# A gated attention and mixture-of-experts layer on one core: where the passages between its stages put five small pieces of work

## The reference, cut to what matters

```
x = x + tanh(g_xattn) * attention(layernorm(x), ctx)       # q, k, v, o of 512 x 512
n = layernorm(x)
probs = softmax(n @ gate_w.T)                              # 8 experts
g, m = top_k(probs per expert, k = 2 * 2048 / 8 = 512)     # 512 tokens for each expert and batch
h = gelu(n[m] @ w1[e])                                     # 512 x 512 by 512 x 2048
out = scatter_add(g * (h @ w2[e]))                         # 512 x 2048 by 2048 x 512
x = x + tanh(g_ffn) * out
```

## Time and profile before

| | us |
|---|---|
| median of 3 runs | 1557.32 |
| lowest and highest | 1556.76, 1558.54 |
| the profiled execution | 1556.92 |
| its span, first to last instruction | 1555.2 |

### The profile page before, as it was taken

The page is one execution under the profiler, slowest core; times in us unless marked ns, Lnnn a source line. Parts: engine busy times, 40 slices in busy tenths (PEclk is TensorE's granted clock), DMA queues, the critical chain, the costliest instruction groups (busy, mean ns, idle before and its releaser), DMA issues.

```text
span 1555.2 us, 20287 instructions
## 1 busy us (share of the span) xinstructions
PE 1498.2 (96%) x7329; PEld 1230.2 (79%) x7329; DVE 1016.6 (65%) x1714; ACT 721.5 (46%) x1270; POOL 589.4 (38%) x554
## 2 busy tenths in 40 slices
PE   6987699999999999999999999999999999999997
PEld 6765477787788888888888888888888888888886
DVE  2677676657766676676667666667667665766543
ACT  2244433355444554454445554554445444554432
POOL 2264555534544044323443244404432344323311
PEclk9998799999999999999999999999999999999999
DMA  7274623533342333344233423334324423342133
GB/s 230 76 242 158 203 89 118 135 127 85 86 123 58 105 88 102 95 88 116 82 109 73 117 78 113 66 97 101 96 89 88 116 81 109 79 111 73 49 71 79
DMA packets 101385, 163.37 MB, mean 105 GB/s; under 512 B 7411, under 2 KB 45315, under 8 KB 101285
## 3 DMA queue, kind: packets, MB, share of 16 engines
q1 hardware_dynamic: 86885, 128.50, 26.5%
q0 software_dynamic: 14400, 33.56, 11.5%
HBM read 128.48 MB, written 33.55 MB: 104 GB/s over the span
## 4 chain that ended last, share of the span: by engine, by line
PE 88%; DVE 7%; DMA 2%; issue 1%; ACT 1%; POOL 1%; SPq 0%; POOLq 0%; DVEq 0%; ACTq 0%
PE bank L1408 42%; PE bank L1294 33%; PE bank L1268 4%; PE bank L1585 2%; PE bank L565 1%; DVE atleast L971 1%; DVE onehot L1468 1%; DMA x_s<-in_x 1%; PE bank L406 1%; PE bank L589 1%; DVE x L840 1%; DVE hid_low L1286 0%; DMA ctx_raw<-in_ctx 0%; PE bank L1457 0%; PE bank L554 0%
## 5 line engine op out<-in xcount | busy, mean ns | idle before, releaser
L1408 PE MATMUL bank<-w2hl,hh 128*128 128x512 f32 x2024 | 628.8, 392 | 0.0
L1294 PE MATMUL bank<-xo,whl 128*128 128x512 f32 x2352 | 544.0, 390 | 3.5 <-DVE mix L1358 2.8
L1294 PEld LDWEIGHTS bank<-xo,whl 128*128 128x128 f32 x2352 | 442.0, 188 | 97.3 <-DVE mix L1358 3.7
L1408 PEld LDWEIGHTS bank<-w2hl,hh 128*128 128x128 f32 x2024 | 376.2, 188 | 75.3
L1408 PE MATMUL bank<-w2hl,hid_low 128*128 128x512 f32 x1012 | 394.0, 389 | 0.0
L1408 PEld LDWEIGHTS bank<-w2hl,hid_low 128*128 128x128 f32 x1012 | 190.1, 188 | 39.8
L1532 POOL DMA_INDIRECT layer_out<-y,slot_row x64 | 104.6, 1634 | 296.7 <-ACT y L1447 281.3
L1222 POOL TENSOR_TENSOR whl<-raw,whl 128x512 fp32r<-128x512 f32 x56 | 81.3, 1452 | 261.1 <-ACT whl L1188 261.1
L1253 DVE TENSOR_TENSOR w2hl<-raw,w2hl 128x512 fp32r<-128x512 f32 x213 | 147.8, 716 | 40.6 <-ACT w2hl L1248 40.6
L1248 ACT ACTIVATE w2hl<-raw 128x512 fp32r<-128x512 f32 x228 | 136.5, 624 | 58.9 <-DMA raw<-in_L_ffn_w 40.1
L1227 POOL TENSOR_TENSOR whl<-wsum,whl 128x512 fp32r<-128x512 f32 x56 | 73.9, 1319 | 183.5 <-ACT whl L1209 183.5
(11 more groups left out here) (230 smaller groups left out, 1792.1 us busy)
## 6 DMA issues: line engine op xcount, KB each, us to landing
raw<-in_L_ffn_w SPq DMA_DIRECT2D x228, 256.0 KB, 2.7
raw<-in_L_ffn_w SPq DMA_DIRECT2D x72, 512.0 KB, 4.9
x_s<-in_x SPq DMA_DIRECT2D x8, 1024.0 KB, 9.5
layer_out<-x SPq DMA_DIRECT2D x8, 1024.0 KB, 10.4
xn_rows<-xn SPq DMA_DIRECT2D x8, 1024.0 KB, 5.2
raw_k<-in_L_xattn_Wk SPq DMA_DIRECT2D x1, 1024.0 KB, 5.5
raw_q<-in_L_xattn_Wq SPq DMA_DIRECT2D x1, 1024.0 KB, 11.3
raw_v<-in_L_xattn_Wv SPq DMA_DIRECT2D x1, 1024.0 KB, 13.4
```

What stands on the lines that cost most here:

```text
L1294: last = pe.matmul(bk[:, :], whl[:, p % 2, part, 2 * w + k, :], xo[:, xpart, x, k, :], start=(not adds and k == 0 and part == HIGH and xpa ...
L1408: last = pe.matmul(Y_BANKS[c][:, :], high if hpart == HIGH else low[:, c * P:(c + 1) * P], w2hl[:, f % 4, part, :], start=(s == 0 and hpar ...
```

## The change

It makes five edits.

1. The low part of w1 pair 0 goes from GpSimd, where it stood ahead of the gathers, to VectorE, ahead of the token splits. The function is renamed `w1_low_part` and takes the engine; GpSimd's low part of pair 1 waits until that of pair 0 is made.
2. On GpSimd the deviations of quarter 6 stand ahead of the four gathers; those of quarter 7 stay behind them.
3. On VectorE the logits of quarters 6 and 7 stand ahead of the fourth chunk's split.
4. TensorE makes the second batch's first count in the output stage of block 0, after its first quarter, like the others; `hidden_pe` loses its parameter.
5. At the change from expert 0 to expert 1, ScalarE's copy of the first product stands behind the high part of w1 pair 1 and ahead of the high part of its sums, and VectorE's low parts of expert 1's first two w2 blocks stand behind its output rows.

```diff
--- before.py
+++ after.py
@@ -766,14 +766,13 @@
                         rows(q, i)
 
 
-            w1_low_pool(pool, 0, 0, 0)
+            deviations(NQ - 2)
             for c in range(NC):
                 gather_pool(pool, 0, 0, c)
-            deviations(NQ - 2)
             deviations(NQ - 1)
             for f in range(2):
                 w2_low_sub(pool, 0, 0, f)
-            w1_low_pool(pool, 0, 0, 1)
+            w1_low_part(pool, 0, 0, 1)
             for q in (NQ - 2, NQ - 1):
                 for i in range(Q):
                     rows(q, i)
@@ -894,10 +893,12 @@
                     mean_out(q)
                 between(q, 3)
                 between(q, 4)
-            for c in range(NC):
+            w1_low_part(dve, 0, 0, 0)
+            for c in range(NC - 1):
                 split_tokens_dve(dve, 0, c)
             logits_out(NQ - 2)
             logits_out(NQ - 1)
+            split_tokens_dve(dve, 0, NC - 1)
 
         def attention_over(eng):
 
@@ -1208,7 +1209,10 @@
             act.wait_ge(w1_sums, pairs_before(e, p) * 3 + 3)
             act.activation(whl[:, p % 2, HIGH, 2 * S1:14, :], wsum[:, :, :], ACT.Copy).then_inc(w1_sum_high, 1)
 
-        def w1_low_pool(pool, e, b, p):
+        def w1_low_part(pool, e, b, p):
+
+            if is_plain(e) and b == 0 and p == 1:
+                pool.wait_ge(w1_low, 1)
             high, low = whl[:, p % 2, HIGH, :, :].bitcast(F32), whl[:, p % 2, LOW, :, :]
             pool.wait_ge(w1_high, pair_no(e, b, p) + 1)
             if is_plain(e):
@@ -1255,7 +1259,7 @@
 
 
 
-        def hidden_pe(pe, b, f, inside=None):
+        def hidden_pe(pe, b, f):
             n = step_no(0, b, f)
             p = f // 2
             if f == 0:
@@ -1269,8 +1273,6 @@
                                      xp[:, b, xpart, k, :],
                                      start=(k == 0 and part == HIGH and xpart == HIGH),
                                      stop=(k == KD - 1 and part == LOW))
-                if k == 1 and inside is not None:
-                    choice_pe(pe, 1, inside)
             last.then_inc(h_sum, 1)
 
         def gelu_act(act, b, f):
@@ -1630,7 +1632,7 @@
         OPERANDS_2 = {7: 0, 9: 1, 11: 2, 13: 3}
 
         def choice_piece(b, f):
-            return f if b == 0 and 1 <= f < N_PIECES else None
+            return f if b == 0 and f < N_PIECES else None
 
         def next_pair(b, f):
 
@@ -1653,7 +1655,7 @@
             for b in range(B):
                 for f in range(KF):
                     if f + 1 < KF:
-                        hidden_pe(pe, b, f + 1, 0 if b == 0 and f == 0 else None)
+                        hidden_pe(pe, b, f + 1)
                     if b == 0:
                         if f == SLOTS_1:
                             slots_pe(pe, 1)
@@ -1680,6 +1682,8 @@
                         operands_high_act(act, 1, OPERANDS_2[f])
                     if f % 2 == 0:
                         w1_high_act(act, *next_pair(b, f))
+                        if b == 1 and f + 2 == KF:
+                            copy_p1_act(act, 1, 0)
                         if next_pair(b, f)[0] == 1:
                             w1_sum_high_act(act, 1, next_pair(b, f)[2])
                     if b == 0 and f == LAST_SLOT:
@@ -1690,7 +1694,6 @@
                 if b == 0:
                     gelu_act(act, 1, 0)
                 else:
-                    copy_p1_act(act, 1, 0)
                     hidden_act(act, 1, 0)
                 for c in (0, 1):
                     output_rows(act, 0, b, c, y_act)
@@ -1698,7 +1701,7 @@
         def plain_dve(dve, own):
             for b in range(B):
                 for f in range(KF):
-                    if choice_piece(b, f) is not None:
+                    if f > 0 and choice_piece(b, f) is not None:
                         choice_dve(dve, own, 1, choice_piece(b, f))
                     if f + 1 < KF:
                         split_hidden_dve(dve, b, f + 1)
@@ -1707,7 +1710,8 @@
                     if b == 1 and f in OPERANDS_2:
                         operands_mix_dve(dve, 1, OPERANDS_2[f])
                     if b == 1:
-                        w2_low_sub(dve, *next_block(b, f))
+                        if next_block(b, f)[0] == 0:
+                            w2_low_sub(dve, *next_block(b, f))
                     else:
                         if f == HOT_1:
                             hot_dve(dve, 0, 1)
@@ -1731,6 +1735,9 @@
                     combine_dve(dve, 1, 0)
                 for c in (2, 3):
                     output_rows(dve, 0, b, c, y_dve)
+                if b == 1:
+                    for f in range(2):
+                        w2_low_sub(dve, 1, 0, f)
 
         def plain_pool(pool):
             for b in range(B):
@@ -1740,7 +1747,7 @@
                     if w2_no(*next_block(b, f)) < W2_EARLY:
                         w2_low_sub(pool, *next_block(b, f))
                     if f % 2 == 0:
-                        w1_low_pool(pool, *next_pair(b, f))
+                        w1_low_part(pool, *next_pair(b, f))
                     if b == 0 and f == GATHER_1:
                         for c in range(NC):
                             gather_pool(pool, 0, 1, c)
@@ -1869,7 +1876,7 @@
             for p in range(NP):
                 new = following_pair(e, p, final)
                 if new is not None:
-                    w1_low_pool(pool, new[0], 0, new[1])
+                    w1_low_part(pool, new[0], 0, new[1])
                 if p == 2:
                     promote_pool(pool, e, 1)
                 if p in GATHER_AT and not final:
```

## The result

| | before | after |
|---|---|---|
| median of 6 runs each, on one chip | 1557.87 | 1547.12 |
| lowest and highest | 1555.69, 1558.56 | 1545.97, 1548.93 |
| the profiled execution | 1556.92 | 1545.97 |
| its span | 1555.2 | 1543.9 |

The ratio is 0.9934, with a 95% interval of 0.9921 to 0.9947: 10.3 us less by the ratio (8.3 to 12.3). The forecast was 1547.5. Five further runs of the same kernel, beside nine more runs of the kernel before, had a median of 1548.59 and a ratio of 0.9944 (0.993 to 0.9957), which is 8.7 us less.

A forecast was written before the change was run, and what follows sets the result against it. TensorE, 88% of the chain, bounds the kernel; gains come only where the chain leaves it or its clock has fallen. -1.9 + 0.1 - 5.5 - 2.5 = -9.8 us from 1556.92: 1547.1, median 1547.5; 8-in-10 range 1544.0 to 1551.0.

The forecast's parts named there:

- The two places named: Passages from attention to expert 0 (150 to 192 us) and from expert 0 to expert 1 (368 to 381 us).
- Part 1: Ahead of the last attention quarter, two VectorE integer operations wait for GpSimd's subtractions; moving these gains 1.9 us.
- rival B: The two integer operations ahead of the last attention quarter are slow by themselves: 1549.4, chance 0.08.
- Part 2: Before expert 0: deviations ahead of the gathers cost 0.1 us; logits ahead of the fourth chunk's split cost 0.
- a hole of 1.34 us: VectorE's gap between third split (172.76) and fourth (174.10), which the six logits operations would fill in about 1.3 us.
- Parts 2 and 3: Expert 0's first hidden blocks: earlier choice and first count one block later start the third hidden block 5.5 us earlier.
- rival A: TensorE's clock falls again after the first hidden blocks, some 1.7 us: 1549.2, chance 0.12.
- Part 4: Passage to expert 1: the first pair's 42 matmuls lose their waits, gaining 2.5 us.
- Rival D: Passage to expert 1 gives nothing, w2's late low parts delaying VectorE's next sums by what was won: 1550.0, chance 0.07.
- three waits: Passage to expert 1: TensorE waits for ScalarE's copy, VectorE's first sum and the third sum, 2.5 us together.
- Rivals E and F: E: expert 0's weight preparation becomes the bound, 1559.5, chance 0.03; F: the change does not act, 1556 to 1557, chance 0.04.
- rival C: Expert 1's later 1.80 us stall goes too, with its clock fall: 3.7 us more, 1543.8, chance 0.06.

The follow-up runs named there:

- the hold: Kernel before with edits 2 and 3, plus GpSimd waiting for the last logits before its first w2 subtraction: median 1553.94, ratio 0.9976.
- the early one-hot: Changed kernel with expert 2's first one-hot matrices made by VectorE one pair of blocks earlier in expert 1: median 1546.82, ratio 0.993.

## Why the prediction was right

**What bounds it.** The two places named were the two that moved: -7.5 us between `part_i` and the third hidden block, -2.4 in the passage to expert 1.

**Part 1** (forecast -1.9): the chain has 0.37 us where it had 2.39, and the stretch shrinks by 1.85 with edit 2's 0.17 inside it. Alone the edit gives 2.02. Putting work back on GpSimd brings the slow operations back, which rules out rival B. The Trainium skill (SBUF — State Buffer, Who interferes with whom) has the lock that I drew on, and reductions outside it. This trace agrees on both: the comparison waited for a subtraction and took 2.09 us instead of 1.09, while the maximum over the logits, a reduction, began at 172.06 beside the subtraction of 171.86 and took 0.28 (before, at 180.06 and beside GpSimd's rows, 0.29).

The two subtractions cost nothing on VectorE, as forecast: they end at 167.67 (166.38 + 1.29), and VectorE still idles 0.87 us before the first token split.

**Part 2** (forecast +0.1 on the gathers, 0 on the split). The gathers pay 0.17 us, measured by undoing it. The logits fit in this profile. But the step "a hole of 1.34 us" was treated as a property of the program when it is one outcome of a race between ScalarE's copies and the fourth chunk. With edits 2 and 3 alone, and with edit 2 undone, the profiled runs went the other way and TensorE waited 5.8 to 6.9 us. In the changed kernel's two profiles it did not happen. This belonged among the rivals, with a price of 3.5 us on edits 2 and 3 alone (38.67 against 35.21 with the hold) and 1.7 on the changed kernel (34.30 against 32.59, with the early one-hot in both).

**Parts 2 and 3 together** (forecast -5.5, measured -5.4). From the first hidden matmul on (the forecast's times less 174.85, those of the chain less 172.19), they compare so:

| | forecast | measured |
|---|---|---|
| count ends | 7.85 | 7.53 |
| both hidden blocks end | 7.75 | 8.11 |
| first hidden split ends | 8.55 | 8.44 |
| stall | 0.8 | 0.37 |
| third hidden block | 11.50 | 11.64 |

Errors of about 0.3 us each met. I forecast waits of the choice for GpSimd at the difference, the product and the candidates. There were three, but not these: the difference (0.94 us in the chain), the candidates (1.19) and the comparison (2.09), which I had left at 1.09, while the product took 0.31. The 24 matmuls took 0.36 us longer at their start than at the clock that I carried over from the earlier trace rows. The windows of the changed kernel (columns as in the earlier trace rows) show where the clock came up:

```profile
172.60:176.50 3.90, 3.90 (x10) 3.03 (x10) 3.40 (x7) 2.38 (x4) 3.90 (x4) 0.50 0.53 165
176.50:180.00 3.50, 3.50 (x15) 2.75 (x14) 3.47 (x3) 1.23 (x2) 3.50 (x4) 0.88 0.02 6
180.00:184.00 4.00, 3.63 (x17) 2.60 (x16) 2.88 (x6) 2.70 (x4) 4.00 (x5) 1.00 0.46 174
```

No fall comes after 0.37 us of stall, nor after 0.89 in the second profile and with the count put back, so rival A is out. What I gave no share to is how the 5.5 divides; I booked it under the moved count. The earlier logits carry 4.8 of it, the first count's place is worth 0.6 on top, and nothing alone.

**Part 4** (forecast -2.5, measured -2.42, alone -2.4). Rival D is out. The copy alone gives nothing, so "three waits" was the right reading: they stand in series, and the second hides what the first would give. The late w2 subtractions (373.61 in the timeline after, 1.28 us for both) held nobody: the next pair is one piece of 42.

**The slower rivals.** Rivals E and F are out: from the third hidden block to expert 1 the stretch is 176.75 us against 176.64, so the preparation of weights did not become the bound, and both passages moved.

**The rest.** The sum was -9.8, the profiled spans differ by 11.3. 0.5 of that is the early stages' spread. 0.3 lies between the first gather and the first hidden matmul, where I had forecast nothing. 1.4 is in expert 1. It is the clock's part of rival C, which I had priced at 1.9 by setting 4.61 us against an undisturbed stage of 2.73: the 1.8 us stall of the earlier trace rows stayed (1.88), but the clock did not fall after it, so the next 12 matmuls took 3.16 us. The granted clock of the kernel before shows the fall:

```profile
408.00:412.00 4.00, 4.00 (x27) 2.81 (x26) 2.11 (x4) 1.89 (x3) 0.00 (x0) 0.59 0.02 4
```

Eleven profiles hold this stall at 1.78 to 1.89 us (all in which the one-hot was not moved). With the kernel before, edit 1, edits 2 and 3 with and without the hold, edit 5 and the copy alone, the 12 matmuls took 4.54 to 4.62 us; with edit 4 alone, both profiles of the changed kernel, and this one with the count back or GpSimd busy, 3.16 to 3.18. The length of the stall doesn't separate the two groups. The four profiles that stand on the changed kernel are all in the fast group, six of the seven others in the slow one, so the edits may have a hand in these 1.4 us; no run shows how, and what decides stays open.

That the median came out 0.4 us from the forecast is partly luck. Of the 11.3 us between the profiled executions, 1.9 (the early stages and the clock in expert 1) have nothing to do with the sum of 9.8, and the second set of runs gives a gain of 8.7 us where the first gives 10.3.

Taken alone, edit 1, edits 2 and 3, edit 4 and edit 5 sum to -8.6 us by their ratios (-2.2, -4.7, -0.8, -0.9), each with some 1.5 us of uncertainty and some 3 together, against 10.3 and 8.7 for the whole: additive within that. The last two can't be told from nothing by their times.

## What to carry to other kernels

An operation that ends each time just as another engine's instruction ends is probably waiting for that engine, and its own duration stands in a row of the same size elsewhere: look there before calling it slow, and give the other engine its work back to show it. Waits in one queue passage stand in series; removing the first can be worth nothing (here 0.04 us) until the next one on the list has been moved too, and one run with only the first move shows it. A hole in a profile is one execution's: ask which landing or release opens it, and price the order in which it stays shut.

## What the runs showed of the hardware

**VectorE and GpSimd.** The logits, candidates, comparison and integer operations of VectorE that met a GpSimd subtraction of 128x512 waited for it to end, however small they were: 0.19 us of logits became 1.2 to 1.3, 0.23 us of integers 0.95 to 1.22. Four such operations of a row of six made it 4 us longer. The reductions beside the same subtractions (0.28 and 0.29 us, at 172.06 and 173.67 after) and a reciprocal (0.25, at 173.99) did not wait. It goes the other way too: before, GpSimd's single subtraction at 191.63 took 2.15 us instead of about 1.25, behind VectorE's comparison of 191.53 to 192.62. And one wait can span several subtractions: in expert 1 after, a VectorE subtraction of 128x512 that takes 0.69 us elsewhere took 3.74 (381.70), beside GpSimd's row of them up to 384.89.

**TensorE's clock.** The same stall of 1.8 to 1.9 us, at the same place, was followed by the 1.2 GHz level in some profiles (12 matmuls in 4.6 us, which is partly at 2.4 GHz) and by none of it in others (3.2 us). Before, the first microsecond behind the stall was still granted 1.00, the next three 0.50 to 0.52. The Trainium skill (TensorE: Matmul & The Clock Gate, HAM oscillation) ties the fall to a long enough idle gap. The stalls of 4.65 and 5.46 us here, which were followed by slow matmuls, and those of 0.37 and 0.89, which were not, agree with it. The 1.8 us stall was followed by both, so its length alone did not decide, and a forecast should price both.

**The spread.** The start of the same instruction 151 us into the program varied by 3.6 us over the profiles (150.94 to 154.55) with nothing changed ahead of it. The fourth gather's chunk reached TensorE between 3.8 us (edit 4 alone) and 6.7 us (the copy alone) after the gather began. This moves the first hidden matmul by 2 us and the hole for the logits with it; whether it is what spreads the runs is not shown. Differences of under 1 us were therefore read from stretches between two landmarks and not from the times.
